# Weight preparation by a fixed list for each engine, and the gate's fold in four partition quarters

## The reference, cut to what matters

```python
x = L0_attn_data                                      # (4, 512, 1024) f32: 2048 tokens
block_mask = mask.reshape(32, 32, 32, 32).astype(f32).sum(axis=(1, 3)) > 0
w_masked = weight * repeat(repeat(block_mask, 32, 0), 32, 1)
x = x + einsum('bsk,nk->bsn', layernorm(x), w_masked)
h = layernorm(x)
logits = h @ W_gate + b_gate                          # 8 experts
_, top_idx = top_k(logits, 2)
y_all = relu(einsum('bsd,edh->bseh', h, W_e) + b_e)
return x + take_along_axis(y_all, top_idx[..., None], axis=2).mean(axis=2)
```

## Time and profile before

| what | us |
|---|---|
| median of the runs | 726.85 |
| the profiled execution | 726.92 |
| its span in the trace | 725.2 |
| TensorE busy in the span | 701.0 (97%) |
| VectorE, ScalarE, GpSimd busy | 329.6, 238.8, 280.1 |
| mean granted clock of TensorE | 0.989 |

### The profile page before, as it was taken

The page is one execution under the profiler, slowest core; times in us unless marked ns, Lnnn a source line. Parts: engine busy times, 40 slices in busy tenths (PEclk is TensorE's granted clock), DMA queues, the critical chain, the costliest instruction groups (busy, mean ns, idle before and its releaser), DMA issues.

```text
span 725.2 us, 11215 instructions
## 1 busy us (share of the span) xinstructions
PE 701.0 (97%) x3599; PEld 569.0 (78%) x3599; DVE 329.6 (45%) x673; ACT 238.8 (33%) x320; POOL 280.1 (39%) x252
## 2 busy tenths in 40 slices
PE   6799999999999999999999999999999999999994
PEld 5258888888877878888888888888888888888883
DVE  4737787888998765336063342143361640000000
ACT  3641212222323134434343333434343434333330
POOL 4312112112645235545353545354453545253430
PEclk9899999999999999999999999999999999999997
DMA  8804454457763338868477577386685764331313
GB/s 317 317 6 175 145 178 172 136 185 271 238 216 143 119 135 235 234 172 235 126 199 236 115 235 161 75 236 202 153 257 134 188 186 88 61 59 30 59 30 58
DMA packets 34501, 118.21 MB, mean 163 GB/s; under 512 B 5776, under 2 KB 5776, under 8 KB 34448
## 3 DMA queue, kind: packets, MB, share of 16 engines
q1 hardware_dynamic: 22032, 80.23, 30.8%
q0 software_dynamic: 11232, 37.23, 25.3%
q10 hardware_dynamic: 1184, 0.04, 0.1%
HBM read 83.40 MB, written 37.75 MB: 167 GB/s over the span
## 4 chain that ended last, share of the span: by engine, by line
PE 85%; DVE 7%; issue 4%; POOL 2%; ACT 1%; POOLq 0%; DVEq 0%
PE psO L334 75%; PE psT L432 5%; PE psG L465 1%; DVE st L680 1%; DVE xr L707 1%; PE psO L392 1%; PE psT L355 1%; DVE st L688 1%; PE psT L378 1%; PE psS L392 1%; POOL w_stage L1051 1%; ACT rows_a L555 0%; PE psT L450 0%; POOL rs L1033 0%; ACT w_stage L560 0%
## 5 line engine op out<-in xcount | busy, mean ns | idle before, releaser
L334 PE MATMUL psO<-slots,xT 128*128 (+1 forms) x1872 | 436.0, 392 | 0.0
L334 PEld LDWEIGHTS psO<-slots,xT 128*128 128x128 f32 x1872 | 348.2, 188 | 70.7
L334 PE MATMUL psO<-wT,xT 128*128 128x512 f32 x768 | 183.9, 395 | 0.0
L334 PEld LDWEIGHTS psO<-wT,xT 128*128 128x128 f32 x768 | 141.5, 188 | 31.4 <-issue 2.6
L1079 POOL DMA_INDIRECT rows_out<-xb,tok_of x37 | 61.4, 1659 | 222.8 <-ACT xb L649 215.5
L834 DVE CAST slots<-raw 128x1024 fp32r<-128x1024 f32 x56 | 50.8, 906 | 192.1 <-PE psO L334 105.0
L649 ACT ACTIVATE xb<-psO 128x512 f32<-128x512 f32 x78 | 46.6, 598 | 253.3 <-PE psO L334 253.3
L1073 POOL TENSOR_TENSOR xT<-x2T,xT 128x1024 fp32r<-128x1024 f32 x38 | 98.0, 2579 | 18.8 <-ACT x2T L628 18.6
L836 DVE TENSOR_TENSOR slots<-raw,slots 128x1024 fp32r<-128x1024 f32 x56 | 79.1, 1412 | 1.9
L590 ACT ACTIVATE psO<-bias_slot 128x512 f32 (+1 forms) x78 | 47.0, 602 | 37.1 <-ACT xb L649 17.3
L1018 POOL TENSOR_SCALAR rs<-mv 128x1 f32<-128x1 f32 x16 | 4.5, 279 | 113.6 <-DVE mv L682 113.6
(11 more groups left out here) (168 smaller groups left out, 455.8 us busy)
## 6 DMA issues: line engine op xcount, KB each, us to landing
raw<-L_ffn_W_e SPq DMA_DIRECT2D x56, 512.0 KB
xb<-data_t SPq DMA_DIRECT2D x16, 512.0 KB, 4.5
x_rows<-x SPq DMA_DIRECT2D x16, 512.0 KB, 5.1
xr<-L_attn_data SPq DMA_DIRECT2D x11, 512.0 KB, 5.7
rows_out<-xr SPq DMA_DIRECT2D x11, 512.0 KB, 2.7
mask_stage<-L_attn_mask SPq DMA_DIRECT2D x8, 512.0 KB, 11.5
w_stage<-L_attn_weight SPq DMA_DIRECT2D x8, 512.0 KB, 13.0
bias_slot<-L_ffn_b_e SPq DMA_DIRECT2D x8, 512.0 KB
```

Source lines behind the costliest of these rows:

```text
L334: last = eng.matmul(psum, xT[:, p, a, kt, :], moving(b, kt), start=(i == 0 and kt == 0 and not seeded), stop=(i == len(PASSES) - 1 and kt ...
```

## The change

It rewrites the lists of the weight preparation and the fold. The loop and the expert stage keep their code.

- GpSimd masks all eight blocks; `MEAN_DVE`, `masked_and_mean` and `w_sum` go. ScalarE takes all eight means and centres, in a list of its own: `mean(r)`, `w_hi(r - 1)`, `centre(r)` up to block 3, then blocks 4 to 7 in an order written out.
- VectorE's list is written out too: `w_lo(r)`, `element_mask(r + 3)`, `sum_mask(r + 4)` for r = 0 to 2, then the masks 6 and 7 around `w_lo(3)` and `x_lo(0)`, then the splits 4 to 7.
- The fold is four products of 256 columns, whose results lie at partitions 0, 32, 64 and 96 of one bank (`psF = psS[:, 0:256]`). VectorE zeroes these columns first. ScalarE copies them out in one instruction, and two transposes over all partitions unfold them, in place of eight over eight partitions.
- The three passes of half 0 stand together behind the fold of block 4 (`PASS_AT = 4`) and `group_sums(7)`. The first pass of half 1 goes ahead of the unfolding.
- `x` of token block 0 is loaded in front of block 4 instead of 3. The warming is (16, 24, 24) in place of (16, 56), with group sums between.

```diff
@@ -190,13 +191,13 @@
         psS = ps("psS", [P, HALF])
 
         psN = psS[:, 0:2 * N_EXP].rearrange("p (a e) -> p a e", e=N_EXP)
-        psF = [psO[0:N_EXP, 1, :], psS[0:N_EXP, :]]
-        psU = psG[:, 64:64 + KT * N_EXP]
+        psF = psS[:, 0:QUARTER]
+        psU = psG[:, 256:512]
 
         def psB(r):
             return psG[:, 128 + NSUB * (r % 4):128 + NSUB * (r % 4 + 1)]
 
-        psW = psG[:, 256:256 + N_EXP]
+        psW = psG[:, 64:64 + N_EXP]
         psM = psS[:, 128:128 + N_LATE + N_EXP]
         psQT = psS[:, 256:256 + P]
         psL = psT[:, 1, KT // 2, 0:2 * N_EXP]
@@ -251,11 +252,10 @@
 
         block = ctx.enter_context(nc.Block())
         NCONST = 21
-        PASS_AT = NT // 2 + 1
-        X0_AT = 3
-        WARM = (16, 56)
-        MEAN_DVE = (2, 5)
-        MEAN_ACT = tuple(r for r in range(NT) if r not in MEAN_DVE)
+        NVCONST = 7
+        PASS_AT = NT // 2
+        X0_AT = 4
+        WARM = (16, 24, 24)
 
 
         @block.sync
@@ -343,6 +343,8 @@
 
             def group_sums(r):
                 eng.wait_ge(c_msum, r + 1)
+                if r >= 4:
+                    eng.wait_ge(c_em, r - 3)
                 eng.matmul(psB(r), group[:], msum[:, r, :], start=True, stop=True).then_inc(c_group, 1)
 
             def transpose_w(r):
@@ -382,41 +384,43 @@
             group_sums(0)
             warm(WARM[1])
             group_sums(1)
-            group_sums(2)
-            for r in range(NT):
-                transpose_w(r)
-                if r == 0:
-                    eng.wait_ge(s_small, 32)
-
-                for n in range(NH):
-                    last = eng.matmul(psF[n], wg[:, r, :], w_stage[:, r, n * HALF:(n + 1) * HALF],
+            warm(WARM[2])
+            def fold_w(r):
+                for q in range(N_QUART):
+                    last = eng.matmul(psF[32 * q:32 * q + N_EXP, :], wg[:, r, :], w_stage[:, r, q * QUARTER:(q + 1) * QUARTER],
                                       start=(r == 0), stop=(r == NT - 1))
                 if r == NT - 1:
                     last.then_inc(c_fold, 1)
-                if r + 3 < NT:
-                    if r + 3 >= 4:
-                        eng.wait_ge(c_em, r)
-                    group_sums(r + 3)
-
-                i = r - PASS_AT
-                if i == 0:
+
+            transpose_w(0)
+            group_sums(2)
+            eng.wait_ge(s_small, 32)
+            eng.wait_ge(s_vconst, NVCONST)
+            fold_w(0)
+            for r in range(1, NT):
+                if r + 2 < NT - 1:
+                    group_sums(r + 2)
+                transpose_w(r)
+                fold_w(r)
+                if r == PASS_AT:
+                    group_sums(NT - 1)
+                    eng.wait_ge(c_xhi, 1)
+                    one_pass(0, psO[:, 0, :], 0, w_half(0))
                     eng.wait_ge(c_wlo, NT // 2)
+                    one_pass(1, psO[:, 0, :], 0, w_half(0))
                     eng.wait_ge(c_xlo, 1)
-                if 0 <= i < len(PASSES):
-                    last = one_pass(i, psO[:, 0, :], 0, w_half(0))
-                    if i == len(PASSES) - 1:
-                        last.then_inc(c_mm, 1)
+                    one_pass(2, psO[:, 0, :], 0, w_half(0)).then_inc(c_mm, 1)
             eng.wait_ge(c_part, 1)
-            eng.wait_ge(c_em, NT)
             eng.matmul(psW, ones[:], wg_part[:], start=True, stop=True)
+            eng.wait_ge(c_whi, NT)
+            one_pass(0, psO[:, 1, :], 0, w_half(1))
             eng.wait_ge(c_fold_out, 1)
-            for kt in range(KT):
-                last = eng.transpose(psU[:, kt * N_EXP:(kt + 1) * N_EXP],
-                                     foldedT[:, kt // (KT // NH), kt % (KT // NH) * P:(kt % (KT // NH) + 1) * P],
-                                     ident[0:N_EXP, 0:N_EXP])
+            for c in range(QUARTER // P):
+                last = eng.transpose(psU[:, c * P:(c + 1) * P], foldedT[:, c * P:(c + 1) * P], ident[:])
             last.then_inc(c_unfold, 1)
             eng.wait_ge(c_wlo, NT)
-            project_half(0, 1)
+            one_pass(1, psO[:, 1, :], 0, w_half(1))
+            one_pass(2, psO[:, 1, :], 0, w_half(1)).then_inc(c_mm, 1)
 
             def transpose_rows(b):
                 eng.wait_ge(l_gather[b % 4], 16 * (b // 4 + 1))
@@ -545,18 +549,15 @@
                     eng.wait_ge(c_mm, NH * (t - 1))
                 eng.activation(xT[:, t % 2, HI, :, :], x_side(t), ACT.Copy).then_inc(c_xhi, 1)
 
+            def mean(r):
+                eng.wait_ge(c_masked, r + 1)
+                if r > 0:
+                    eng.wait_ge(c_mean, r)
+                eng.activation(rows_a[:], w_stage[:, r, :], ACT.Copy, scale=-1.0 / D,
+                               accum_out=minus_mean[:, r:r + 1]).then_inc(c_mean, 1)
+
             def centre(r):
-
-                if r in MEAN_ACT:
-                    k = MEAN_ACT.index(r)
-                    eng.wait_ge(c_masked_p, k + 1)
-                    if k > 0:
-                        eng.wait_ge(c_mean_a, k)
-                    eng.activation(rows_a[:], w_stage[:, r, :], ACT.Copy, scale=-1.0 / D,
-                                   accum_out=minus_mean[:, r:r + 1]).then_inc(c_mean_a, 1)
-                    eng.wait_ge(c_mean_a, k + 1)
-                else:
-                    eng.wait_ge(c_mean_d, MEAN_DVE.index(r) + 1)
+                eng.wait_ge(c_mean, r + 1)
                 eng.activation(w_stage[:, r, :], w_stage[:, r, :], ACT.Identity,
                                bias=minus_mean[:, r:r + 1]).then_inc(c_wm, 1)
 
@@ -564,17 +565,26 @@
                 eng.wait_ge(c_wt, r + 1)
                 eng.activation(wT[:, HI, :, r * P:(r + 1) * P], psT[:, w_half_of(r), :, :], ACT.Copy).then_inc(c_whi, 1)
 
+            mean(0)
             centre(0)
-            centre(1)
-            for r in range(NT):
+            for r in range(1, PASS_AT):
+                mean(r)
+                w_hi(r - 1)
+                centre(r)
+            mean(PASS_AT)
+            centre(PASS_AT)
+            w_hi(PASS_AT - 1)
+            x_hi(0)
+            w_hi(PASS_AT)
+            for r in range(PASS_AT + 1, NT):
+                mean(r)
+                if r == NT - 1:
+                    w_hi(r - 2)
+                centre(r)
+            for r in range(NT - 2, NT):
                 w_hi(r)
-                if r + 2 < NT:
-                    centre(r + 2)
-                if r + 1 == X0_AT:
-                    x_hi(0)
             eng.wait_ge(c_fold, 1)
-            eng.activation(foldedT[:, 0, :], psF[0], ACT.Copy)
-            eng.activation(foldedT[:, 1, :], psF[1], ACT.Copy).then_inc(c_fold_out, 1)
+            eng.activation(foldedT[:], psF, ACT.Copy).then_inc(c_fold_out, 1)
 
             def seed_half(b, slot, n):
 
@@ -669,6 +679,7 @@
             eng.wait_ge(s_vconst, 5)
 
             eng.scalar_tensor_tensor(first_col[:], spare[:], float(P), first_col[:], ALU.mult, ALU.add).then_inc(s_vconst, 1)
+            eng.memset(psF, 0.0).then_inc(s_vconst, 1)
 
             def stats1(t):
                 eng.wait_ge(l_xr[t % 3], 16 * (t // 3 + 1))
@@ -854,41 +865,34 @@
                 eng.wait_ge(c_group, r + 1)
                 eng.tensor_scalar(emask[:, r, :], psB(r), 0.0, None, ALU.is_gt).then_inc(c_em, 1)
 
-            def masked_and_mean(r):
-
-                eng.wait_ge(c_em, r + 1)
-                eng.wait_ge(s_w[r], 16)
-                rows = w_stage[:, r, :].rearrange("p (g s) -> p g s", s=SUB)
-                eng.scalar_tensor_tensor(rows, rows, 1.0, emask[:, r, :].unsqueeze(2).to_broadcast([P, NSUB, SUB]),
-                                         ALU.mult, ALU.mult, accum_out=w_sum[:, r:r + 1]).then_inc(c_masked_d, 1)
-                eng.wait_ge(c_masked_d, MEAN_DVE.index(r) + 1)
-                eng.tensor_scalar(minus_mean[:, r:r + 1], w_sum[:, r:r + 1], -1.0 / D, None, ALU.mult).then_inc(c_mean_d, 1)
-
             for r in range(3):
                 sum_mask(r)
                 element_mask(r)
-            for r in range(NT):
-                if r + 2 in MEAN_DVE:
-                    masked_and_mean(r + 2)
-                if r + 3 < NT:
-                    sum_mask(r + 3)
+            sum_mask(3)
+            for r in range(3):
                 w_lo(r)
-                if r + 3 < NT:
-                    element_mask(r + 3)
-                if r + 1 == X0_AT:
-                    x_lo(0)
+                element_mask(r + 3)
+                sum_mask(r + 4)
                 if r == 0:
                     eng.wait_ge(s_small, 32)
                     eng.tensor_reduce(wg_part[:], wg[:].rearrange("p k e -> p e k"), AX.X, ALU.add).then_inc(c_part, 1)
+            element_mask(6)
+            sum_mask(7)
+            w_lo(3)
+            x_lo(0)
+            element_mask(7)
+            for r in range(4, NT):
+                w_lo(r)
 
             eng.wait_ge(c_unfold, 1)
-            folded = psU.rearrange("p (k e) -> p k e", e=N_EXP)
```

(21 more changed lines are left out.)

## The result

The kernel after the change takes 714.62 us in the median of four executions against 726.7 us before: a ratio of 0.984, 95% interval 0.9823 to 0.9858, so 12.1 us faster. The profiled execution took 714.62 us with a span of 712.9. In a second set of measurements it was 714.33 against 726.68 (0.9834, interval 0.982 to 0.9847).

The account below looks back on a forecast made before the run. An order on VectorE, then TensorE's work, partly at half clock, was taken to bound the start. Half 1 of token block 0 ending at 46.6 instead of 58.4 saves 11.8: 726.92 - 11.8 = 715.1 us, range 713.4 to 720.0.

Parts of the forecast that it names:

- What bounds the kernel: Start of the kernel: bound by an order on VectorE, then TensorE's own work, 6 us of it at half clock.
- the price of zero: VectorE's loop at token block 1, nearer to TensorE by some 2 us: costs nothing; without cover at most 2 us.
- VectorE's list (part 3): Sums and element masks ahead of late splits: mask 7 summed from 27.1 to 28.3; added zeroing 0.3 us.
- The passes (part 4): TensorE's three passes of half 0 together behind group sum 7, running from 28.6 to 34.3.
- The fold (part 5): Four quarter products replace two: 1.07 us per fold if only neighbours overlap, between 0.45 and 1.81.
- Behind the passes (part 6): Transposes and folds 5 to 7, unfolding and half 1's passes after 34.3: half 1 ends at 46.6 instead of 58.4.
- the rival of full overlap: Folds of 0.45, transposes 7 waiting for ScalarE's centring 7, half 1 ending near 45.5: 714.0; inside the 0.51 case.
- The rule on drains: Changing TensorE's tiling mode drains it: two drains of 0.3 us per row block, blocks 5 to 7, add 1.8: 716.9.
- The clock: Rival: shorter folds leave TensorE lighter between 13 and 28, its clock dips, middle 4.9 us: 720; chance 0.18.
- The sign of no idle time above 2 us: Evidence expected if right: TensorE has no idle time above 2 us between 13 and 45.
- The serial fold: Rival: the fold's quarters don't overlap, each fold stays about 1.8 us, gain 8.7: 718.2; chance 0.24.
- the slow clock: Rival: clock falls near 14 us and stays, half 1 ends near 69.4, 11 us later: 738; chance 0.04.

Follow-up runs that it names:

- the probe: Kernel before plus 24 unread fp32 products of the fold's shape in its warm-up, in three patterns of partition quarters; one execution, 733.29 us.
- the version beyond both: Changed kernel with first pass ahead of group sum 7, third behind fold 7, block 7 masked and summed on VectorE: 713.09 us, ratio 0.9815.
- three filled kernels: Unused matmuls added behind folds 0 to 3: changed kernel (ratio 0.9827), changed kernel with VectorE's old list (718.98 us), the version beyond both (713.82 us).
- the order alone: Changed kernel with the fold of before, two products of 512 columns in two banks, unfolding ahead of half 1's first pass: 719.03 us, ratio 0.9891.

## Why the prediction held, point by point

- **What bounds the kernel.** Right. Half 1 ends 12.4 us earlier and the span is 12.3 shorter, so what follows token block 0 gave back 0.1 us at most. The x split of token block 1 started at 44.40 and was done at 45.6, with TensorE asking for it at 47.6, so the price of zero stands.
- **VectorE's list (part 3).** Right: mask 7's sum started at 27.19 (27.1 expected). The zeroing, taken at 0.3, moved the first group sum from 7.12 to 7.38. The old list in the changed kernel put mask 6's sum back to 27.92.
- **The passes (part 4).** 28.87 to 34.43, against 28.6 to 34.3. Putting them together was worth some 0.8 us, which is too little for the runs to tell from nothing.
- **The fold (part 5).** The one term that was mis-sized. I took 1.07 us between 0.45 and 1.81; it is 0.54 with its neighbours and 0.50 in the probe (four times 0.124). The step that failed is the one from "fill the same quarter one after the other" to five steps of 0.21: if a product's two records held up the next quarter, the probe's four-quarter pattern would cost 0.27 each, and it cost 0.124. The low bound of 0.45 was nearly met. The Trainium skill, TensorEngine Tiling (Array Packing), Theoretical Speedup, gives up to 4x for a dimension of 32 or less. The probe agrees with 3.6x (0.445 against 0.124).
- **Behind the passes (part 6).** Here the forecast was near in part by luck. With the short fold the chain left TensorE, as the rival of full overlap had it, but it waited for something else: transposes 7 started at 37.77 behind VectorE's low split of block 5 (done at 37.64), which I had fitting beside TensorE's work, while the centring of block 7, which the rival named, was done at 37.40. A second wait, for ScalarE's split of block 7, stood in front of half 1: 0.64 us from the column-sum product to the pass, where the version beyond both took 0.14. That rival's half 1 ended at 45.5 and mine at 46.6; it was 45.96. Three folds were 1.6 us too long in my sum (3 x 0.53), and the two waits that it lacked give back 0.9 (0.42 + 0.50), which leaves the error of 0.6.
- **The rule on drains.** The 1.8 us priced for it did not come. In the probe eight products in four quarters and the step to the full-size matmul behind them take 0.99 us, and in the changed kernel four products and that step take 0.54; an estimate from the two gives 0.11 for a product and 0.09 for the step. The fold of before had the same step: its first product took 0.86 us to the second, and the second 0.96 to the pass behind it, as TensorE's timeline of before has it.

```profile
43.33 1.02 PE L392 MATMUL psO<-w_stage,wg 128*8 128x512 f32 x2
44.19 1.02 PE L392 MATMUL psS<-w_stage,wg 128*8 128x512 f32 x2
45.15 2.12 PE L334 MATMUL psO<-wT,xT 128*128 128x512 f32 x8
```

The Trainium skill, TensorEngine Tiling (Array Packing), Key Properties, has a change of tiling mode drain the engine. The traces show no cost of it beyond the 0.1 us that the wide products had too.
- **The clock.** The profiled execution shows 1.00 all along, but the rival was not empty. In the changed kernel's other profiled execution the clock fell near 24 us with no gap of TensorE above 1.81 us since 13 us, while I had argued from a gap of 4.68. The sign of no idle time above 2 us was missed by little, 2.06, and in the execution where the clock held. I priced a dip at 4.9 us. The one that was traced cost nothing, since TensorE waited there anyway; the highest execution, 716.43 against 714.62, had the lower mean clock (0.990 against 0.994) but no trace, so that its 1.8 us are the clock is likely and not shown.
- **The serial fold and the slow clock** did not occur.

## What to carry to other kernels

Read for each engine which instruction the bound engine waits for and what stands in front of it in its list; two mask sums put behind an x split cost 5 us here, the late sums and a dip of the clock together. When an engine is relieved by several edits, look for what is late next, since the last of the fold's gain went into waits for other engines. Products with few output rows can be put into different partition quarters of one bank and then overlap almost fully (3.6 times as fast here), fp32 ones too. And look at when the loads land before two kernels are compared: masks landed more than 1 us apart in kernels that issue them alike.

## What the runs showed of the hardware

- Four fp32 products of 8 x 256 in four partition quarters take 0.50 us instead of 1.78 in one quarter, and two quarters halve the time (0.230 against 0.445).
- TensorE's clock fell to the 1.2 GHz level in work with gaps of 1 to 2 us: about the fall the changed kernel's execution had TensorE busy 2.19 of 4.00 us from 20 to 24. Where fillers raised that to 3.50, fourteen executions of three kernels lay within 0.23 us of their fellows. The fall does not come in every execution: the version beyond both had 2.02 of 4.00 in the same stretch of its profile and stayed at 1.00.
- All three filled kernels received mask 4 later. Its load, issued at 5.7, took 13.5 us in the filled kernel against 12.3 in the changed one:

```profile
L272 SPq DMA_DIRECT2D mask_stage<-L_attn_mask x1: 707/707/707, 5.7 to 5.7; - x1
...
DMA to landing us min/median/max: 12.3/12.3/12.3
```

```profile
L272 SPq DMA_DIRECT2D mask_stage<-L_attn_mask x1: 739/739/739, 5.7 to 5.7; - x1
...
DMA to landing us min/median/max: 13.5/13.5/13.5
```

  What the late ones share is when an instruction fetch (0.02 MB, its own DMA queue) comes. It starts at 16.3 to 17.0 us in the three filled kernels and at 14.7 in the probe's, and in these four mask 4 landed at 19.1 to 19.2. In the other ten traces it starts at 17.7 or later, and mask 4 landed at 17.8 to 18.1. Mask 7 shows the same: in the two kernels with the fetch at 25.4 to 25.5 (the order alone, the fold left out) it landed at 25.6 to 25.7, in all others at 26.7 or later. So the masks behind the fetch come 1 us or more later than where they stand ahead of it. That the fetch itself is the cause was not tried by an edit.
